# Attention of two batches as one chain of eight groups, with the first group's weights split in the experts' loop

## What is computed

```python
xn = _layernorm(x, axis=-1)
x = x + _L0_attn_ref(xn, w_q, w_kv, w_dense) + _L0_ffn_ref(xn, Wr, br, W1, W2, Ws1, Ws2)
# attention: 16 query heads of 128 in 4 groups, one key/value head per group, causal
scores = jnp.einsum('bqgpd,bkgd->bgqpk', q, k) * SCALE
ctx = jnp.einsum('bgqpk,bkgd->bqgpd', softmax(masked scores), v)
return jnp.einsum('bse,eh->bsh', ctx, w_dense)
# experts: 32 of 256 hidden units, 6 per token (from 4 of 8 groups), gated
h = jnp.square(jax.nn.relu(xf @ w1.T)) @ w2.T;  acc = acc + g[:, None] * h
shared = jnp.square(jax.nn.relu(xn @ Ws1.T)) @ Ws2.T
```

## Time and profile before

| | us or share |
|---|---|
| median of 3 runs | 1680.87 |
| profiled execution | 1680.17 |
| its span, first to last instruction | 1677.9 |
| PE busy | 1571.7 (94%) |
| DVE, ACT, POOL busy | 69%, 51%, 17% |
| mean granted TensorE clock | 0.976 of full |
| HBM read and written | 122.77 and 56.36 MB |

### The profile page before, as it was taken

The page is one execution under the profiler, slowest core; times in us unless marked ns, Lnnn a source line. Parts: engine busy times, 40 slices in busy tenths (PEclk is TensorE's granted clock), DMA queues, the critical chain, the costliest instruction groups (busy, mean ns, idle before and its releaser), DMA issues.

```text
span 1677.9 us, 31729 instructions
## 1 busy us (share of the span) xinstructions
PE 1571.7 (94%) x8812; PEld 1341.6 (80%) x8813; DVE 1151.8 (69%) x2335; ACT 858.1 (51%) x1767; POOL 292.9 (17%) x542
## 2 busy tenths in 40 slices
PE   6898899999999969999999999986999999999996
PEld 5776788888888857888888888865788888888885
DVE  6587665565565627857957957862795885885885
ACT  4454566666666624544545545532553453454453
POOL 0002333333333301011011011020100101101101
PEclk9899899999999989999999999997999999999999
DMA  5391666766676631012012012122111201201102
GB/s 203 131 407 40 201 215 210 240 214 222 216 229 218 210 103 45 20 57 63 19 56 63 19 56 82 39 90 100 45 32 45 63 23 52 63 21 54 39 7 82
DMA packets 61734, 180.14 MB, mean 107 GB/s; under 512 B 6736, under 2 KB 6864, under 8 KB 56912
## 3 DMA queue, kind: packets, MB, share of 16 engines
q1 hardware_dynamic: 36800, 107.84, 18.4%
q0 software_dynamic: 16640, 54.54, 11.7%
q10 hardware_dynamic: 8208, 16.78, 2.6%
HBM read 122.77 MB, written 56.36 MB: 107 GB/s over the span
## 4 chain that ended last, share of the span: by engine, by line
PE 89%; DVE 4%; issue 2%; ACT 2%; DMA 1%; DVEq 0%; ACTq 0%; POOLq 0%; SPq 0%
PE bank L595 8%; PE bank L597 8%; PE bank L596 8%; PE bank L885 7%; PE ps_s L595 6%; PE ps_s L597 6%; PE ps_s L596 6%; PE ps_s L873 5%; PE ps_s L874 4%; PE ps_s L868 4%; PE ps_s L766 4%; PE ps_s L770 3%; PE ps_s L767 3%; PE ps_s L781 3%; PE ps_s L785 3%; PE ps_s L782 3%
## 5 line engine op out<-in xcount | busy, mean ns | idle before, releaser
L1192 ACT ACTIVATE probs<-ps_s,negmax 128x128 f32<-128x128 f32 (+7 forms) x256 | 189.6, 741 | 177.8 <-DVE negmax L1573 176.8
L1222 DVE TENSOR_TENSOR pT_lo<-bank,pT_hi 128x512 fp32r<-128x512 f32 x288 | 196.3, 686 | 76.5 <-ACT pT_hi L1200 75.1
L1200 ACT ACTIVATE pT_hi<-bank 128x512 fp32r<-128x512 f32 x288 | 168.9, 596 | 149.9 <-PE bank L885 148.3
L1573 DVE TENSOR_REDUCE negmax<-ps_s 128x1 f32<-128x128 f32 (+7 forms) x256 | 188.9, 749 | 11.4 <-PE ps_s L874 8.9
L397 POOL TENSOR_TENSOR settled<-ident 128x1 f32<-128x1 f32 x192 | 54.3, 283 | 769.7 <-DVE acc L1600 760.1
L595 PE MATMUL ps_s<-xT_hi,wa_hi 128*128 128x512 f32 x384 | 156.5, 408 | 26.3 <-DVE wa_lo L1222 26.3
L885 PE MATMUL bank<-ident,probs 128*128 128x128 f32 x1152 | 167.8, 273 | 2.0 <-DVE pT_lo L1222 2.0
L885 PEld LDWEIGHTS bank<-ident,probs 128*128 128x128 f32 x1152 | 139.6, 141 | 29.7 <-DVE pT_lo L1222 2.4
L597 PE MATMUL ps_s<-xT_hi,wa_lo 128*128 128x512 f32 x384 | 153.1, 399 | 0.0
L596 PE MATMUL ps_s<-xT_lo,wa_hi 128*128 128x512 f32 x384 | 152.7, 398 | 0.0
L868 PE MATMUL ps_s<-kT_hi,qT_hi 128*128 128x512 f32 (+3 forms) x384 | 138.6, 361 | 6.1 <-ACT probs L1192 3.3
(11 more groups left out here) (190 smaller groups left out, 3695.4 us busy)
## 6 DMA issues: line engine op xcount, KB each, us to landing
eraw<-we SPq DMA_DIRECT2D x37, 1024.0 KB, 6.3
expert_outputs<-ysb SPq DMA_DIRECT2D x111, 256.0 KB
araw<-wa SPq DMA_DIRECT2D x40, 512.0 KB, 4.2
expert_outputs<-comb ACTq DMA_DIRECT2D x1, 16384.0 KB, 49.8
normed_tokens<-xn SPq DMA_DIRECT2D x4, 1024.0 KB, 6.3
out<-acc SPq DMA_DIRECT2D x2, 2048.0 KB, 8.2
res<-x SPq DMA_DIRECT2D x2, 1024.0 KB, 6.6
acc<-x SPq DMA_DIRECT2D x2, 1024.0 KB, 14.1
```

The lines of the kernel that those rows point to most:

```text
L1192: act.activation(probs[:, i % 2, a, 0:keys], src, ACT.Exp, bias=negmax[:, i % 2, a:a + 1], accum_out=rowsum[:, i % 2, a:a + 1]).then_inc(e ...
L1200: act.activation(pT_hi[:, blk % RING, :], ps_t[blk % 2][:, :], ACT.Copy).then_inc(pt_hi_ready, 1)
L1222: dve.tensor_tensor(out_, whole, upper.bitcast(F32), ALU.subtract).then_inc(signal, 1)
L1573: dve.tensor_reduce(negmax[:, i % 2, a:a + 1], src, AX.X, ALU.max, negate=True).then_inc(max_ready, 1)
```

## The change

- The two unused "experts" at the end of the list become the first 4096 columns (pieces 0 to 3) of the first attention group's weights, and the slots 2 and 3 of the experts' weights are now the same memory as the attention's `wa_hi` and `wa_lo`. `FIRST_ORDER` has no W steps any more. Before the loop SP loads pieces 3 and 4.
- The buffers are laid out anew. `FIRST` starts without `room_free`: PE waits for the last weight split and the last transposed tokens, and before the second projection for the last output copy. ACT waits for `room_free` after `FIRST`.
- The two batches form one chain: `FIRST`, a loop of seven `GROUP`, one `LAST`. Batch 1's turned rows are stored in DRAM in the opening (4 MB) and loaded in the fourth group, after its projections. ACT waits for these stores before it overwrites the rows.
- In the fourth group SP stores each tile of `acc` after its last dense sum, and reloads it with the other batch's residual and shared sum; the last group's tiles are stored one by one too. DVE waits for the first two reloads at C0 and for all eight at D0.
- In the experts' loop the bounds are carried in registers and read two experts ahead, after PE's `hidden_tile`; the four tests for the gathered slot become two nested ones. Before the loop some waits are removed and one for `z_out` is moved up.
- POOL has 7 more increments at the start.

```diff
-FIRST_ORDER = ("W0 W1 W2 K0 K1 P0 P1 Q00 Q01 Q02 Q03 S00 E00 S01 E01 N00 X S02 E02 N01 S03 E03 N02 N03")
+FIRST_ORDER = ("K0 K1 P0 P1 Q00 Q01 Q02 Q03 S00 E00 S01 E01 N00 X S02 E02 N01 S03 E03 N02 N03")
...
-        hi_slot = lambda s: (w_hi01, w_hi23)[s // 2][:, s % 2, :]
-        lo_slot = lambda s: (w_lo01, w_lo23)[s // 2][:, s % 2, :]
+        hi_slot = lambda s: w_hi01[:, s, :] if s < 2 else wa_hi[:, (s - 2) * W_COLS:(s - 1) * W_COLS]
+        lo_slot = lambda s: w_lo01[:, s, :] if s < 2 else wa_lo[:, (s - 2) * W_COLS:(s - 1) * W_COLS]
...
+        def slot_of(e):
+            return (e + SLOTS // 2) % SLOTS
...
-        def over_experts(eng, body, row=0):
+        def over_experts(eng, body):
+            lo_reg = eng.alloc_register()
+            hi_reg = eng.alloc_register()
+            eng.reg_mov(lo_reg, 0)
+            eng.reg_mov(hi_reg, pair_bound(eng, 1))
             with eng.Fori(0, E // SLOTS) as es:
-                lo = pair_bound(eng, es * SLOTS, row)
+                lo = eng.snap(lo_reg, min_val=0, max_val=MAXT)
+                hi = eng.snap(hi_reg, min_val=0, max_val=MAXT)
                 for s in range(SLOTS):
-                    hi = pair_bound(eng, es * SLOTS + s + 1, row)
-                    body(es * SLOTS + s, s, lo, hi, es)
-                    lo = hi
-        def attend_groups(eng, attend, turn):
-            attend(FIRST, turn * GROUPS)
-            with eng.Fori(0, GROUPS - 1) as g:
-                attend(GROUP, turn * GROUPS + g, g)
-            attend(LAST, turn * GROUPS + (GROUPS - 1), GROUPS - 1)
+                    lo, hi = hi, body(es * SLOTS + s, s, lo, hi, es)
+                eng.reg_mov(lo_reg, lo)
+                eng.reg_mov(hi_reg, hi)
+        def attend_groups(eng, attend):
+            with eng.Fori(0, GROUPS_ALL - 1) as n:
+                attend(GROUP, n)
+            attend(LAST, GROUPS_ALL - 1)
...
+                if s == 0:
+                    for c in range(2):
+                        sp.wait_ge(xlo_ready, (c + 1) * HALF)
+                        for i, part in enumerate((xT_hi, xT_lo)):
+                            sp.dma_start(xT_d[c, i, :, :].rearrange("p (k n) -> p k n", k=KD),
+                                         part[:, :, c * C:(c + 1) * C].bitcast(F32)).then_inc(xT_out[c], 16)
...
-            sp.wait_ge(ew_lo, (NSH + E + 2) * WP)
-            sp.wait_ge(mx_lo, last + 1)
-            sp.sem_inc(room_free, 1)
             for half in range(2):
                 sp.wait_ge(y_stored[half], past(((last + (1 - half)) // 2) * 16))
                 sp.sem_inc(y_free, 1)
-            for s in range(2):
-                sp.wait_ge(eraw_in[s], ALL_IN[s])
             sp.sem_inc(room_free, 1)
-            load_piece(0, 0, 2)
-            with sp.Fori(0, B) as turn:
-                b = turn
-                with sp.Fori(0, GROUPS - 1) as g:
-                    n = turn * GROUPS + g
-                    load_piece(n, g, 3)
-                    load_piece(n, g, 4)
-                    for c in range(3):
-                        load_piece(n + 1, g + 1, c)
-                n = turn * GROUPS + (GROUPS - 1)
-                load_piece(n, GROUPS - 1, 3)
-                load_piece(n, GROUPS - 1, 4)
-                with sp.If(turn == 0):
+            def store_tile(b, t):
+                sp.wait_ge(dense_added, past(((b + 1) * GROUPS - 1) * NT + t + 1))
+                if t == 0:
+                    sp.wait_ge(comb_added, past(((b + 1) * GROUPS - 1) * NCOMB))
+                if t == NT - NT // GROUPS:
+                    sp.wait_ge(comb_added, past((b + 1) * GROUPS * NCOMB))
+                if b < B - 1:
+                    sp.wait_ge(out_done, past(t * 16))
+                sp.dma_start(outb[:, b * NT + t, :], acc[:, t, :]).then_inc(out_done, 16)
+            def load_z(t):
+                sp.wait_ge(out_done, past((t + 1) * 16))
+                sp.wait_ge(z_ok, past(GROUPS * (16 * NT) + t * 16))
+                sp.dma_start(acc[:, t, :], z_d[t * P:(t + 1) * P, :]).then_inc(z_ok, 16)
+            def switch_tiles(lo, hi):
+                for t in range(lo, hi):
+                    if t:
+                        sp.wait_ge(dense_added, past((GROUPS - 1) * NT + t + 1))
+                        load_z(t - 1)
+                    store_tile(0, t)
+            with sp.Fori(0, GROUPS_ALL - 1) as n:
+                load_piece(n + 1, 0)
+                load_piece(n + 1, 1)
+                with sp.If(n == GROUPS - 1):
+                    sp.wait_ge(z_out, 16)
+                    for c in range(2):
+                        sp.wait_ge(xT_out[c], 32)
                     sp.wait_ge(proj_ready, GROUPS * PROJ)
-                    for half in range(2):
-                        sp.dma_start(xn_again[half], xn_b[:, NT + half * (NT // 2):NT + (half + 1) * (NT // 2), :]).then_inc(xn_in, 16)
-                    load_piece(n + 1, 0, 0)
-                    load_piece(n + 1, 0, 1)
-                sp.wait_ge(dense_added, past((turn + 1) * (GROUPS * NT)))
-                sp.wait_ge(comb_added, past((turn + 1) * (GROUPS * NCOMB)))
-                sp.dma_start(outb[:, bass.ds(b * NT, NT), :], acc[:, :, :]).then_inc(out_done, 16)
-                with sp.If(turn == 0):
-                    sp.wait_ge(out_done, past(16))
-                    sp.wait_ge(z_out, 16)
-                    sp.dma_start(acc[:, :, :], z_d.rearrange("(t p) d -> p t d", p=P)).then_inc(z_in, 16)
-                    load_piece(n + 1, 0, 2)
-            sp.wait_ge(out_done, past(16 * B))
+                    for c in range(2):
+                        for i, part in enumerate((xT_hi, xT_lo)):
+                            sp.dma_start(part[:, :, c * C:(c + 1) * C].bitcast(F32),
+                                         xT_d[c, i, :, :].rearrange("p (k n) -> p k n", k=KD)).then_inc(xT_ok, 16)
+                    switch_tiles(0, 2)
+                with sp.Else():
+                    sp.sem_inc(xT_ok, 64)
+                    sp.sem_inc(z_ok, 16 * NT)
+                load_piece(n + 1, 2)
+                with sp.If(n == GROUPS - 1):
+                    switch_tiles(2, 4)
+                load_piece(n + 1, 3)
+                load_piece(n + 1, 4)
+                with sp.If(n == GROUPS - 1):
+                    switch_tiles(4, NT)
+                    load_z(NT - 1)
+                    sp.wait_ge(xT_ok, past((GROUPS + 1) * 64))
+                    sp.wait_ge(z_ok, past((GROUPS + 1) * (16 * NT)))
+            for t in range(NT):
+                store_tile(B - 1, t)
+            sp.wait_ge(out_done, past(16 * NT * B))
...
+            pool.sem_inc(xT_ok, 64)
+            pool.sem_inc(z_ok, 16 * NT)
+            pool.sem_inc(aw_hi, 3)
+            pool.sem_inc(aw_lo, 3)
+            pool.sem_inc(araw_in[0], 32)
+            pool.sem_inc(araw_in[1], 16)
...
-                for slot in range(XG):
-                    with pe.If((p + 1) % XG == slot):
-                        transpose_gathered(slot, p + 1)
+                q = p + 1
+                with pe.If(q // 2 % 2 == 0):
+                    with pe.If(q % 2 == 0):
+                        transpose_gathered(0, q)
+                    with pe.Else():
+                        transpose_gathered(1, q)
+                with pe.Else():
+                    with pe.If(q % 2 == 0):
+                        transpose_gathered(2, q)
+                    with pe.Else():
+                        transpose_gathered(3, q)
...
+                hidden_tile(lo, slot_of(s))
+                after = pair_bound(pe, e + 2)
...
+                            pe.wait_ge(xT_ok, past((n + 1) * 64))
+                        if isinstance(n, int) and n == 0 and j == 1:
+                            pe.wait_ge(y_copied, last + 1)
...
-            pe.wait_ge(room_free, 2)
-            with pe.Fori(0, B) as turn:
-                with pe.If(turn == 1):
-                    pe.wait_ge(xn_in, 32)
-                    for t in range(NT):
-                        if t >= 2:
-                            pe.wait_ge(xr_lo, t - 1)
-                        half, at = divmod(t, NT // 2)
-                        for k in range(KD):
-                            mm = pe.transpose(ps_t[t % 2][:, k * P:(k + 1) * P],
-                                              xn_again[half][:, at, k * P:(k + 1) * P], ident[:, :])
-                        mm.then_inc(xr_ready, 1)
-                    pe.wait_ge(xr_lo, NT)
-                attend_groups(pe, attend_pe, turn)
+            pe.wait_ge(ew_lo, (NSH + E + 1) * WP + 2)
+            pe.wait_ge(mx_lo, last + 1)
+            attend_pe(FIRST, 0)
+            attend_groups(pe, attend_pe)
...
+                    act.wait_ge(xT_out[t // HALF], 32)
...
+            for e in range(2):
+                act.wait_ge(eraw_in[e], ALL_IN[e])
+            attend_act(FIRST, 0)
+            act.wait_ge(room_free, 1)
+            attend_groups(act, attend_act)
...
-                        at = g * (NT // GROUPS) + j // TOPK
```

(45 more changed lines are left out.)

144 lines of the change are left out of this document (71 added, 73 removed).

## The result

The changed kernel takes 1599.4 us (median of 4 runs, 1599.03 to 1600.37), the one before 1680.95 beside it (4 runs, 1679.23 to 1682.16). The ratio is 0.9516, with the interval 0.95 to 0.9533: 81.5 us saved, where 63.6 were forecast and the range ended at 1605. The profiled execution is 1600.37 with a span of 1598.6.

A forecast was written before the change was run, and what follows sets the result against it. PE was taken as the bound, busy for 94% of the span, so savings must close holes in its stream: 1680.17 - 14.8 - 36.6 - 4.4 - 8.0 + 0.6 = 1617.0 us, as a median about 1617.3, range 1605 to 1630.

The forecast's parts named there:

- Part 4: Experts' loop: reading bounds two experts ahead closes PE's holes at experts' ends, -8 us, bounds -17 and +5.
- the whole of the holes, -17: Experts' loop: the most it could save, from 393.24 us busy of 410, 16.8 us of holes.
- The other holes: Experts' loop, experts' ends away from the loop's turns: 0.3 us off for some 9 holes, 2.7 us.
- The cap of 16.8 us: Experts' loop from 180 to 590 us: PE's idle time, taken as all the holes it has.
- The rule of instruction fetch: Loop turns: a taken branch outside the fetched window stalls; the 1.29 us would stay, saving some 3 us smaller.
- Rival B: Experts' loop: tests and reads together were the cost, nearly all holes go, -13 to -17 us, 1608 to 1612; chance 0.13.
- Part 2: Turn between batches: fifth group follows after the same 126.57 us instead of 163.15, -36.6 us, bounds -33 to -37.
- Its tightest place: Turn: last tile's store and reload take 5 to 8 us within 16.4 us, hidden with 8 us left.
- Part 1: Seam from experts to attention: hole closed 12.4, clock kept 2.3, earlier loads 0.1, -14.8 us, bounds -12 to -16.
- the 0.4 us left for leaving the loop: Seam: part of the 12.84 us hole expected to remain, sized like the smaller holes at an expert's end, 0.37.
- Part 3: End: only tile 7's store remains after the last sum, 3.7 us instead of 8.1, -4.4 us.
- Part 5: Opening: 7 more POOL start increments, about 0.08 us each, delay SP's first load and all after it, +0.6 us.

The follow-up runs named there:

- `b_read2`: Kernel before the change plus one more late read of a bound, value unused, on PE at each of 32 experts: 1702.81 us, ratio 1.012.
- `b_bounds`: Kernel before the change with only the bounds kept in registers and read two experts ahead on all engines: 1659.19 us, ratio 0.9872.
- `b_both`: Kernel before the change with bounds read two experts ahead into registers and nested slot tests, nothing else: 1655.98 us, ratio 0.9851.
- `b_tests`: Kernel before the change with only two nested tests for the gathered slot in place of four in a row: 1680.05 us, ratio 0.9993.
- `a_whole`: Changed kernel with the first batch's sums stored and the others reloaded in one piece at the turn, not by tile: 1613.73 us, ratio 0.9605.
- `a_gates2`: Changed kernel with the gates' searches moved to the seam, first behind the key tiles, second spread over three query tiles: 1595.33 us, ratio 0.9498.
- `a_gates`: Changed kernel with both batches' gate searches on DVE moved from the opening to the seam, around the two key tiles: 1596.25 us, ratio 0.9498.
- `a_room`: Changed kernel with PE waiting at the seam for the loop's last store, as before the change: 1606.93 us, ratio 0.9559.
- `a_end`: Changed kernel with the last batch stored in one piece at the end instead of tile by tile: 1604.39 us, ratio 0.9549.

## Why the prediction was wrong, point by point

**Part 4, the loop, is the step that failed.** Its mechanism was right (the late read of the bound on PE), its size was not: -8 was put down, -23.4 measured, and its bound "the whole of the holes, -17" didn't hold either. Without that miss the time would have been inside the range. Its terms:
- The read was priced at 0.3 us, "nearer the read that is shown", which is DVE's 0.23. PE's measures 0.69 (`b_read2`), or some 0.65 by itself, close to the other bound, 0.63. The wish to take the price from a shown row led to the row of another engine; the difference of two rows on PE itself, 1.29 - 0.66, was nearly the price. That is partly luck, since the 0.66 is a hole of 0.90 us in steps, at one of the experts that lose more than most.
- At the turns 0.45 each was to go, 3.1 in all; their holes of 1.52 to 1.77 us go nearly whole, 11.0 to 0.6.
- The other holes were counted from pieces that stood out in the chain, some 9, for 2.7 us. All 25 other experts lose, 12.7 us together, and nearly all of it goes. Over the whole loop 26.6 falls to 4.2.
- 2.0 was for DVE's and ACT's reads. The steps from the output matmuls to the transposes behind them have 2.0 us over the median before and 0.0 after, which fits; but no run moves these reads by themselves.
- The tests were put at nothing. Alone they give 0.8, which can't be told from nothing; with the reads moved it is 3.2.
- The cap of 16.8 us came from idle time, which leaves out the start of every hole.

With the reads moved, `b_bounds` and `b_both` have no such wait as the 1.29 at a turn. In `b_bounds` the first tile behind a turn has some 0.2 us more than that of another expert, for the jump back and the register moves: the hole of 1.53 was two reads of 0.65 and this. The rule of instruction fetch that was weighed there (the Trainium skill, "Runtime: NRT & Kernel Launch", instruction fetch mechanics) would have kept the 1.29; no run shows such a stall. By the Trainium skill's "Advanced Engine Details and Errata", Control Flow Timing, two fewer tests were an estimated 24 us; `b_tests` measures 0.8, with an interval that takes in zero (-2.9 to +0.5 us). Rival B gave the right direction, but it put the tests and the reads together as the cause, and its 13 to 17 us were under the same cap.

**Part 2, the turn**, was right in the way shown: even 126.57 us. Its tightest place was the tiles' exchange, as said, and `a_whole` shows what it is worth. That the size fits to 0.1 us is partly luck. The 163.15 of the earlier trace rows is one execution; in the four kernels above with the same turn as before the step is 159.8 to 160.8 us, by which the change would save 33.3 to 34.2.

**Part 1, the seam**, was right in its hole and in the first fall of the clock; the 0.4 us left for leaving the loop didn't show. It measured 16.6 instead of 14.8, since the kernel before has a second fall in it, which the forecast didn't read. Its chain behind the first scores:

```profile
638.93 0.64 PE bank L885 x4
639.57 0.43 PE ps_s L595
640.00 0.43 PE ps_s L596
...
642.13 0.43 PE ps_s L595
```

Seven matmuls and a part of one, 7 x 0.20 + 0.08 = 1.5 us, which the profiled execution of the changed kernel doesn't have. Hole 12.84, clock 2.3 and 1.5 make 16.6. As the other kernels show, this last piece comes and goes.

**Part 3, the end**, had the store right (0.41 + 2.02), but put 0.3 us before its issue and 1.0 for SP's last waits. From the sum's end to the end of the span it is 2.4 us in all, so neither shows, and 5.7 were saved.

**Part 5, the opening**, had the increments right: SP's first load is 0.55 us later (2.83 for 2.28), and PE's first matmul 0.72. The other 2.4 us are not the change's as far as the runs show: kernels with the same opening have the first expert matmul at 172.35, 172.93, 174.32, 174.35 and 174.52 (that of before), and at 173.52, 174.50, 174.78 and 175.48 (that of the change). The means are 173.7 and 174.6, and the 172.35 that the forecast started from is the lowest of its five. A part of what differs is how many matmuls between 26 and 32 us take 0.43 rather than 0.23: five in the kernel before and eleven in the changed one, 1.2 us, though the granted clock is given as 1.00 there. The rest stays open.

## What to carry to other kernels

A value that PE's sequencer reads from SBUF with a short queue was worth a hole of some 0.7 us on average here, so read it a step ahead, behind long work, and keep it in a register; then look for what the early read lies behind. Price a wait from rows on the same engine, even if they have no better name than "issue", measure it from start to start, and count all of its places, not only those that stand out. A step that was read in one execution only can be 3 us off, as the turn was. Before a large transfer is called hidden, cut it so that each piece can go as soon as its data are done: at the turn this was worth 14 us, at the end 5.

## What the runs showed of the hardware

- One more read of a value by PE's sequencer in front of a short queue costs 0.69 us (`b_read2`), 0.60 to 0.69 at the experts where nothing else is lost; DVE's read shows as 0.23.
- PE's idle time in a profile leaves out the first 0.24 us of a hole behind a transpose of 128 columns (record 0.27 us, next start after 0.03), and 0.16 behind a matmul of 256 columns (0.28 and 0.12). Steps from start to start show the hole whole (26.6 against 15 us of waits).
- Around the first scores PE has two holes of some 1.5 us. Behind the second the granted clock fell in `a_gates2` and the kernel before, in `a_gates` and `a_room` already behind the first, and it stayed in the changed kernel, `a_end` and `a_whole` with the same two holes (1.41 and 1.63 us of idle time). The fall costs 1.5 to 1.7 us, so that single profiled executions differ by as much. After a hole of 3.6 us (`a_room`) and of 12.84 it fell too; with none it stayed.
- In the changed kernel a 256 KB store of `acc` lands in 3.1 us in the median; one of 2 MB takes 7.3 us (`a_whole`) to 8.2.
